# Local attention plus quantized feed-forward on one core: score groups in one piece, attend steps in pairs, first row tiles turned on TensorE, new order on all engines

## What is computed

```python
qkv = xn @ w_qkv                                  # 512 -> 1536, 8 heads of 64
# windows of 4 tokens, one every 2 tokens; softmax inside a window
dots = einsum('bnqhd,bnkhd->bnhqk', q, k) * 512**-0.5
o = einsum('bnhqk,bnkhd->bnqhd', softmax(dots), v)
y = o @ w_out + b_out
out.at[:, idx].add(y)                             # windows overlap: a token adds up two of them
# ffn: weights and activations quantized to 4-bit values in blocks of 16 and back
h = silu(fp4(xn) @ fp4(w_gate).T) * (fp4(xn) @ fp4(w_up).T)
ffn = fp4(h) @ fp4(w_down).T                      # 512 -> 1408 -> 512
```

## Time and profile before

| | |
|---|---|
| time, median of 3 executions (lowest, highest) | 2207.1 us (2204.0, 2210.7) |
| the profiled execution: its time; its span | 2204.8 us; 2202.7 us |
| PE busy | 2148.9 us |
| DVE, POOL, ACT busy | 1663.7, 1219.0, 656.9 us |
| first block of PE (`q0`) starts | 33.12 us |
| first feed-forward product on PE starts | 829.19 us |

### The profile page before, as it was taken

One profiled execution on the slowest core, in us unless ns is written; L12 is line 12 of the kernel. 1 busy time (PEld: TensorE's weight loads), 2 busy tenths in 40 slices (PEclk: granted clock), 3 DMA queues, 4 the chain that ended last, 5 costly groups with the idle time before them and its releaser, 6 DMA issues.

```text
span 2202.7 us, 46918 instructions
## 1 busy us (share of the span) xinstructions
PE 2148.9 (98%) x16712; PEld 1037.8 (47%) x16712; DVE 1663.7 (76%) x3108; ACT 656.9 (30%) x1009; POOL 1219.0 (55%) x877
## 2 busy tenths in 40 slices
PE   4999999999999989999999999999999999999999
PEld 1544444544444444444444444444444444444444
DVE  7877877787787666877878778787787777878774
ACT  2342433333343322222222222222222232222221
POOL 3256767666665554555555555555555555555553
PEclk9999999999999999999999999999999999999999
DMA  9656656575766544333333333433334333343333
GB/s 267 189 122 175 157 142 175 133 191 133 177 149 167 136 166 111 82 87 83 78 90 80 87 83 78 94 75 87 86 80 91 77 83 89 77 92 74 87 74 68
DMA packets 449418, 251.82 MB, mean 114 GB/s; under 512 B 367282, under 2 KB 373938, under 8 KB 449300
## 3 DMA queue, kind: packets, MB, share of 16 engines
q1 hardware_dynamic: 448404, 246.99, 46.1%
q10 hardware_dynamic: 576, 2.10, 0.2%
q0 software_dynamic: 320, 0.97, 0.2%
HBM read 99.01 MB, written 59.77 MB: 72 GB/s over the span
## 4 chain that ended last, share of the span: by engine, by line
PE 75%; POOL 10%; issue 9%; DVE 2%; DMA 1%; SPq 0%; ACT 0%; POOLq 0%; DVEq 0%; ACTq 0%
PE acc L978 10%; PE prj L1350 7%; PE ops L1350 7%; PE acc L1331 5%; PE acc L1335 5%; PE acc L1332 5%; PE prj L978 3%; PE ops L1352 3%; PE prj L1352 3%; PE sps L1333 2%; PE acc L1334 2%; PE sps L1336 2%; PE acc L1336 2%; PE sps L1334 2%; PE acc L1333 2%
## 5 line engine op out<-in xcount | busy, mean ns | idle before, releaser
L978 PE MATMUL acc<-late 128*128 128x512 f16 x2304 | 516.8, 380 | 11.0 <-DMA late<-xh 10.9
L978 PEld LDWEIGHTS acc<-late 128*128 128x128 f16 x2304 | 218.4, 98 | 270.7 <-issue 16.5
L209 POOL TENSOR_TENSOR qk<-qk,xh 128x1408 f32<-128x1408 f32 x64 | 165.6, 2588 | 230.1 <-DVE qk L246 230.1
L1225 DVE SCALAR_TENSOR_TENSOR qk<-acc,row_gains,xh 128x512 f32<-128x512 f32 x64 | 48.0, 751 | 260.2 <-ACT xh L1290 260.2
L204 POOL TENSOR_TENSOR qk<-qk,xh 128x1024 f32<-128x1024 f32 (+1 forms) x128 | 177.3, 1386 | 111.2 <-DVE xh L225 111.2
L214 POOL TENSOR_TENSOR v<-qk,v 128x1408 f16<-128x1408 f32 x64 | 183.0, 2859 | 100.3 <-ACT v L256 100.3
L1350 PE MATMUL prj<-late,qk 128*128 128x512 f16 x704 | 214.6, 379 | 0.7 <-DMA qk<-v 0.7
L1350 PE MATMUL ops<-late,qk 128*128 128x512 f16 x704 | 214.6, 379 | 0.0
L256 ACT ACTIVATE v<-qk 128x1408 f16<-128x1408 f32 x64 | 88.1, 1377 | 367.3 <-POOL qk L209 367.3
L1331 PE MATMUL acc<-late,turned 128*128 128x512 f16 x512 | 194.0, 379 | 0.4 <-DVE qk L1225 0.4
L1335 PE MATMUL acc<-late,turned 128*128 128x512 f16 x512 | 194.1, 379 | 0.0
(11 more groups left out here) (158 smaller groups left out, 4440.0 us busy)
## 6 DMA issues: line engine op xcount, KB each, us to landing
normed<-late SPq DMA_DIRECT2D x64, 256.0 KB, 3.0
res<-in_L_attn_x SPq DMA_DIRECT2D x64, 256.0 KB, 2.9
attended<-res SPq DMA_DIRECT2D x64, 256.0 KB, 2.5
raw<-normed SPq DMA_DIRECT2D x64, 256.0 KB, 2.7
v<-attended SPq DMA_DIRECT2D x64, 256.0 KB, 2.7
out<-v SPq DMA_DIRECT2D x64, 256.0 KB, 2.0
late<-in_L_attn_x SPq DMA_DIRECT2D x62, 256.0 KB, 3.8
ready<-turned SPq DMA_DIRECT2D x36, 256.0 KB
```

The costliest lines, as they stand in the source:

```text
L209: pool.tensor_tensor(blocks(v), blocks(v), spread(s[3]), ALU.mult).then_inc(q["valued"], 1)
L978: last = pe.matmul(out, lhsT, rhs, start=(at == 0), stop=(at == n - 1))
```

## The change

- `scores(b, g)` now makes all three tiles of a group in one go: 96 matmuls, with one set of waits ahead (copies of `q`, `packed` for the edge tile, `masked` of the group before). Its place in PE's program is chosen by group.
- `attend` steps come in pairs (`PAIRS`): both of a pair go to different halves of `ops`, only the first waits for ACT's copies (`o_out`), and ACT copies both once the second is done. The edge tile (`a4`) is alone.
- The first four row tiles of batch 0 are turned by PE: `T0` to `T3`, 8 transposes each of 128x128 float16 against `eye` into the idle PSUM banks of `sps` and `ops`; ACT copies each into `xt` (`y0` to `y3`). SP's `t0` to `t3` of batch 0 fall away.
- In the last batch, the output blocks go to `prj` and `acc[2]` in turn, and each waits for the `final` two before it.
- The order strings of all five engines are new; some waits follow (`spread_weights` and `turn_weights` of a tile 0; `first_rounder`; `acc_free`).

```diff
+PAIRS = [(0, 1), (0, 1), (2, 3), (2, 3), (4, 4), (5, 6), (5, 6), (7, 8), (7, 8)]
...
+    def out_bank(b, i):
+        return acc[2] if isinstance(b, int) and b == B - 1 and i % 2 else prj
...
-            pool.wait_ge(p_turned, at(b, ATT, a - 2))
+            pool.wait_ge(p_turned, at(b, ATT, a - 2 if a else -1))
...
+        def rows_turned(b, i):
+            act.wait_ge(flipped, i + 1)
+            act.activation(xt[:, :, :, i * P:(i + 1) * P], flip[i], ACT.Copy).then_inc(xt_in[i], 16)
...
-            act.wait_ge(pv_done, at(b, ATT, a))
-            src = ops[:, :, 0:2 * P].rearrange("p g (c q) -> p c g q", c=KC)
+            act.wait_ge(pv_done, at(b, ATT, PAIRS[a][1]))
+            src = ops[:, :, (a - PAIRS[a][0]) * 2 * P:(a - PAIRS[a][0] + 1) * 2 * P].rearrange("p g (c q) -> p c g q", c=KC)
...
+        def turn_first_rows(b, i):
+            pe.wait_ge(c_in, 32)
+            pe.wait_ge(xlo_done, at(b, TPB, i))
+            for a in range(2):
+                for k in range(KC):
+                    last = pe.transpose(flip[i][:, a, k, :], xh[:, i, a, k * P:(k + 1) * P], eye[:, :])
+            last.then_inc(flipped, 1)
...
+        def scores(b, g):
+            tiles = order[GT * g:GT * g + GT]
+            pe.wait_ge(qkv_out, at(b, QKV, max(q_use(8 * (n // 4) + 7) for n in tiles if n != EDGE)))
+            if EDGE in tiles:
                 pe.wait_ge(packed, at(b, 4, 3))
+            pe.wait_ge(masked, at(b, NG, g - 1))
...
-            pe.wait_ge(o_out, at(b, ATT, a - 1))
+            if a == PAIRS[a][0]:
+                pe.wait_ge(o_out, at(b, ATT, a - 1))
...
-            pe.wait_ge(final, at(b, TPB, i - 1))
-            three_products(prj[:, :], [((oh[:, i % 4, 0, k], oh[:, i % 4, 1, k]),
+            if isinstance(b, int) and b == B - 1:
+                pe.wait_ge(final, at(b, TPB, max(i - 2, -1)))
...
+            else:
+                pe.wait_ge(final, at(b, TPB, i - 1))
+            three_products(out_bank(b, i)[:, :], [((oh[:, i % 4, 0, k], oh[:, i % 4, 1, k]),
...
-                "p6' s5 v4 s4 a0 v5 a1 s6 p7' s7 v6 s8 v7 a2 q0+ q1+ q2+ a3 q3+ q4+ q5+ a4 q6+ q7+",
+                "v4 v5 v6 s1 p6' v7 s2 p7' a0 a1 q0+ q1+ a2 a3 q2+ q3+ q4+ q5+",
+                "q6+ q7+ a4 v0+ v1+ p0 v2+ s0+ p1 a5 a6 p2 v3+ q8+ q9+ q10+ p3 q11+ p4 a7 a8 q12+ q13+ q14+ q15+ p5",
```

More of the change, by code:

```diff
@@ L90 @@
 GATE_AT, UP_AT = [20, 28, 0], [24, 4, 8]
-FIRST_OF, LAST_OF = [0, 3, 6], [2, 4, 8]
 DOWN_AT = [32, *range(11, 20), 3]
@@ L317, in attention @@
     acc, prj, sps, ops = shared.acc, shared.prj, shared.sps, shared.ops
+    flip = [bank.bitcast(F16).rearrange("p (a k t) -> p a k t", a=2, k=KC)
+            for bank in (sps[:, 0, :], sps[:, 1, :], ops[:, 0, :], ops[:, 1, :])]
+    flipped = sem("flipped")
+    def out_bank(b, i):
+        return acc[2] if isinstance(b, int) and b == B - 1 and i % 2 else prj
     w_in, o_in, c_in, b_in = [sem(f"w_in{k}") for k in range(KC)], sem("o_in"), sem("c_in"), sem("b_in")
@@ L754, in turn_weights @@
             dve.wait_ge(p_spread, at(b, ATT, a))
-            dve.wait_ge(pv_done, at(b, ATT, a - 2))
+            dve.wait_ge(pv_done, at(b, ATT, a - 2 if a else -1))
             dve.transpose(pt[:, a % 2].rearrange("p h q -> p (h q)"),
@@ L779, in finish @@
             dve.wait_ge(biased, at(b, TPB, i))
-            dve.scalar_tensor_tensor(res[:, i % 4, :], prj[:, :], sc[:, 5:6], res[:, i % 4, :],
+            dve.scalar_tensor_tensor(res[:, i % 4, :], out_bank(b, i)[:, :], sc[:, 5:6], res[:, i % 4, :],
                                      ALU.mult, ALU.add).then_inc(final, 1)
@@ L947, in first_rounder @@
         def first_rounder(b, k):
+            if k == 1:
+                act.wait_ge(rows.q["rounded"], 1)
             rounder(act, rows.q, rows.raw[:, k, :], rows.rounder, k)
@@ L955, in scalar @@
         batches(act,
[8 rows of a table removed]
-                {"x": high_rows, "q": qk_out, "v": v_out, "e": exponential, "o": attended, "h": out_high,
[8 rows of a table added]
+                {"x": high_rows, "y": rows_turned, "q": qk_out, "v": v_out, "e": exponential, "o": attended, "h": out_high,
                  "B": unit_rounder, "H": high_unit, "W": weights_high, "U": out_weights_high,
@@ L1014, in scores @@
             hold(pe, held)
[L1015 to L1026, removed]
@@ L1027, in scores @@
-            if n == LAST_OF[g]:
-                last.then_inc(s_done, 1)
+            for i, tile in enumerate(tiles):
+                for h in range(HEADS):
+                    r = slice(DH * (h % 2), DH * (h % 2) + DH)
+                    for j in range(P // BLK):
+                        if tile == EDGE:
+                            q = qke[r, h // 2, 8 * j:8 * j + 8, :].rearrange("p n t -> p (n t)")
+                            k = qke[r, KC + h // 2, 8 * j:8 * j + 8, :].rearrange("p n t -> p (n t)")
+                        else:
+                            t = slice(tile * P + j * BLK, tile * P + (j + 1) * BLK)
+                            q, k = qk[r, h // 2, t], qk[r, KC + h // 2, t]
+                        to = i * P + h // 2 * BLK
+                        last = pe.matmul(sps[j * BLK:(j + 1) * BLK, h % 2, to:to + BLK], q, k,
+                                         start=True, stop=True)
@@ L1030, in attend @@
+            last.then_inc(s_done, 1)
         def attend(b, a):
+            half = (a - PAIRS[a][0]) * 2 * P
             tile = order[a]
@@ L1042, in attend @@
                     r = slice(2 * BLK * g, 2 * BLK * (g + 1))
-                    last = pe.matmul(ops[DH * (h % 2):DH * (h % 2) + DH, g, h // 2 * DH:(h // 2 + 1) * DH],
+                    last = pe.matmul(ops[DH * (h % 2):DH * (h % 2) + DH, g,
+                                         half + h // 2 * DH:half + (h // 2 + 1) * DH],
                                      vals[r, h * DH:(h + 1) * DH], pt[r, a % 2, h % 2 * (HEADS // 2) + h // 2, :],
@@ L1049, in project_out @@
             pe.wait_ge(o_lo, at(b, TPB, i))
-            pe.wait_ge(final, at(b, TPB, i - 1))
-            three_products(prj[:, :], [((oh[:, i % 4, 0, k], oh[:, i % 4, 1, k]),
+            if isinstance(b, int) and b == B - 1:
+                pe.wait_ge(final, at(b, TPB, max(i - 2, -1)))
+                if i == 1:
+                    pe.wait_ge(qkv_out, at(b, QKV, QKV - 1))
+            else:
+                pe.wait_ge(final, at(b, TPB, i - 1))
+            three_products(out_bank(b, i)[:, :], [((oh[:, i % 4, 0, k], oh[:, i % 4, 1, k]),
                                                (wo[:, 0, k], wo[:, 1, k])) for k in range(KC)]).then_inc(proj_done, 1)
@@ L1076, in tensor @@
         batches(pe,
[6 rows of a table removed]
-                {"q": project_qk, "v": project_v, "s": scores, "a": attend, "p": project_out, "M": column_tops, "W": out_ready,
[6 rows of a table added]
+                {"q": project_qk, "v": project_v, "s": scores, "a": attend, "p": project_out, "T": turn_first_rows,
+                 "M": column_tops, "W": out_ready,
                  "F": first_products})
@@ L1123, in feed_forward @@
     dps = [shared.ops[:, 1, :], shared.prj[:, :]]
-    acc_free = [ended.copied, ended.copied + ended.masked, ended.masked + ended.evacuated]
+    acc_free = [ended.copied, ended.copied + ended.masked + ended.projected, ended.masked + ended.evacuated]
     def await_all(engine, ends):
```

## The result

The changed kernel takes 2228.4 us (2225.3 to 2231.4), the kernel before 2206.0 us in the same comparison: a ratio of 1.0098, 95% interval 1.0077 to 1.0120. It is 1% slower, where 1.3% faster was forecast.

What follows compares the result with a forecast made beforehand. PE was taken as the bound in both stages, busy 2148.9 of 2202.7 us. Terms of -6.8 + 2.0 - 12.6 - 1.9 - 4.8 - 5.0 = -29.1 us led to a median of 2178.0 us, range 2164 to 2194.

Steps and rivals of the forecast that it cites:

- Loop waits: In the loop, ACT's copy `q7+` behind `h2`: chain about 7.5 us against 7.8 on PE; nothing lost on balance, 0.
- Attend pairs: Four pairs of attend steps a batch, 0.06 us saved in each, 32 times: -1.9 us, from -3.8 to +4.8.
- Scores in one piece: Three merged score pieces a batch take PE 5.55 us against 7.12, over 8 batches: -12.6 us, from -6.7 to -16.2.
- Rival (a): Even pace inside a merged score piece fails over 96 matmuls, so only turns count: 2185 us; chance 0.22.
- Fewer turns: PE turns from float16 blocks to small float32 pieces 52 times less, 0.093 us each: -4.8 us.
- Start: `q0` no longer waits for DMA transposes, starting at 26.3 us instead of 33.1: -6.8 us, from -4.8 to -7.8.
- Rest of batch 0: After the earlier first block, PE waits for ACT's copies, late loads and DVE's chain: +2.0 us, 0 to +5.
- The end: In the last batch two banks remove `final` waits; of 8.0 us of waits 3.0 stay: -5.0 us, -2 to -8.
- Rival (b): New waits in the loop, on ACT's copies, cost 1.5 to 3 us in each of six iterations: 2187 to 2196; chance 0.15.
- (d): Slower than before: in the loop `h2` comes so late that PE waits over 6 us an iteration: 2214 and up; chance 0.05.

## Why the prediction was wrong

- **Loop waits (0, from -6 to +10): the step that failed.** It looked for the narrow place at the copy of `q7` and priced what happens there; PE waited for ACT's copy 0.8 us in all. The place that decided was on no list: `w6`, behind `X2` and `R2`. It cost 16.8 us of waits and most of the 13.8 at half pace; moving it and `f1` gave some 24 us back.
- **Attend pairs (-1.9): the same error from PE's side.** The term priced the joint between two records and not the cover that a pair takes away. In the earlier trace rows blocks stand between the attend steps; side by side, the second needs its weights 0.6 us behind the first. The joint itself was priced too high: in the changed kernel an undisturbed pair takes 1.09 us, where two steps apart take 1.26, so 0.17 saved and not 0.06:

```profile
773.02 1.16 PE L1069 MATMUL ops<-pt,v 64*64 64x64 f32 x64
774.11 7.94 PE L995 MATMUL acc<-late 128*128 128x512 f16 x36
```

Waits and issue gaps inside pairs took that back: with `w6` and `f1` moved, the attend steps take 50.4 us, 5.8 of them waits and gaps, against 48.3 and 0.9 before.
- **Scores in one piece (-12.6).** A second step that failed. The pace held for two of the three groups: 1.75 to 1.9 us where nothing disturbs, 1.70 to 1.85 forecast; the second takes 2.1. Over all groups PE's score time without gaps fell by 6.5, half of the term. And the issue gaps, 22.7 us more than before with those at the jump, were in no term. Most of them end in mid-block, so reading the records of a single score piece couldn't show them. Rival (a) spoke of a drained queue ahead of PE, inside the piece and for 7 us only.
- **Fewer turns (-4.8).** 114 pieces became 63, at the price of the earlier trace rows; the ledger closes with it, but no run shows it alone.
- **Start (-6.8).** Right: -7.7 at `q0`, -6.0 to -6.3 where it is done alone. **Rest of batch 0 (+2.0, up to +5):** right alone, where 4.4 of 6.3 arrive in the time; in the changed kernel batch 0 lost some 7.5 more, which its groups in three pieces gave back.
- **The end (-5.0, from -2 to -8).** The waits for `final` fell as said, but what PE then waits for, ACT's copies and POOL's low part, takes more than the 3.0 us left for it: -1.7 in the run with start and end alone.
- **The rivals.** Rival (b) named the kind (1.5 to 3 us in each iteration) but not the place, and no rival had two such costs together; that a wait of 2.9 costs another 1.4 by the clock is in none. By (d)'s arithmetic it would have taken 6 us an iteration at one place; here it was 4.0 net, from several.

That the whole change isn't bad in itself, the run at 2183.5 shows: with a few steps in other places, and with 9 of its 24 score groups back in three pieces, it comes within 6 us of the forecast 2178.

## What to carry to other kernels

Where a change puts two consumers of a chain side by side, or moves a step on a filler engine, walk every producer of the second one back through each engine's list, filler steps included; a cover of one block may be all that there was. Price a wait of PE of 2 to 3 us at more than its length, for the clock behind it: here one of 2.9 cost 1.4 more, and one of 1.9 (456.23 in the run with `w6` moved) cost 1.7 more. And spread small float32 matmuls: 24 pieces of 384 records cost 24 us of gaps, which mostly don't stand at the piece and have no releaser.

## What the runs showed of the hardware beyond that

- PE's instructions come in transfers of 16384 bytes, of some 217 instructions each by the estimate above. Small float32 matmuls use up as many in 1.0 us (384 records in 1.78), 12 float16 products of 512 columns only a ninth of it (24 records) in 2.59.
- Three joined tiles with waits of their own take 2.1 to 3.1 us in the loop, with one set of waits 1.8 to 2.1, three apart, each behind a block, 2.07. This fits a register wait that hides behind a block but not behind a score piece; no run changes the waits alone.
- DVE's small operations on 128x32 elements took 1.19 and 1.30 us (459.98 and 461.09, above) while POOL ran its own two at 459.87; in the run with `w6` moved, with POOL idle, the same two took 0.18 and 0.23. Over the whole trace of the changed kernel, the 24 of each that began while POOL was busy took 1.08 to 1.31, the 12 that didn't 0.18 to 0.24. The Trainium skill, "GPSIMD Engine Reference", section "1. Specifications", says that GpSimd shares its SBUF interfaces with VectorE, and that they get in each other's way in some of VectorE's modes and where its instruction has two inputs in SBUF. These rows agree, and so does the 1.14 of the earlier trace rows, an addition of two inputs. But other small operations beside POOL stayed short (the reciprocal at 0.34 with and without), and what decides was not tried.
